# Where the first graph layer's accumulator clear, offset table, norm and state store run in a two-block graph kernel

## What is computed

```
x_in = layernorm(x)                               # the state, 3125 x 256
ew = edge_attr @ edge_w + edge_b                  # 100000 x 256
for l in range(3):
    residual = x_in
    msg = relu(x_in[src] * ew)
    out = 0
    for i in range(3):                            # edge types
        h = segment_sum(msg * (type == i), dst) / max(count_i, 1)
        out = out + h @ weights[l, i]
    out = out + x_in @ roots[l] + biases[l]
    x_in = residual + relu(out)
x = x + x_in
```

## Time and profile before

| | us |
|---|---|
| median of three runs | 7416.21 |
| the three runs | 7399.02, 7418.02, 7416.21 |
| profiled execution, device time | 7403.44 |
| its span in the trace | 7401.6 |

### The profile page before, as it was taken

The page is one execution under the profiler, slowest core; times in us unless marked ns, Lnnn a source line. Parts: engine busy times, 40 slices in busy tenths (PEclk is TensorE's granted clock), DMA queues, the critical chain, the costliest instruction groups (busy, mean ns, idle before and its releaser), DMA issues.

```text
span 7401.6 us, 95264 instructions
## 1 busy us (share of the span) xinstructions
PE 4706.3 (64%) x19009; PEld 2793.2 (38%) x19009; DVE 4623.4 (62%) x10963; ACT 2409.1 (33%) x5954; POOL 4497.2 (61%) x4196
## 2 busy tenths in 40 slices
PE   6599822223388887526676667666665766666588
PEld 2255411111244444314444436333333633333365
DVE  7877755555566667626666655666665566666553
ACT  0188700000166663014444442222221222222131
POOL 0000177777677778877777762777776277777600
PEclk9899955555599998758888878777776877777789
DMA  4000177777665553236666682666667376766700
GB/s 111 18 0 0 35 227 224 228 226 231 176 152 152 152 152 73 57 95 211 210 209 210 210 174 94 208 211 212 211 208 174 95 211 211 211 208 210 174 26 18
DMA packets 506841, 1150.06 MB, mean 155 GB/s; under 512 B 115695, under 2 KB 244306, under 8 KB 506497
## 3 DMA queue, kind: packets, MB, share of 16 engines
q0 software_dynamic: 187648, 458.07, 24.6%
q1 hardware_dynamic: 271844, 551.41, 22.5%
q10 hardware_dynamic: 47136, 138.12, 6.6%
HBM read 864.81 MB, written 281.13 MB: 155 GB/s over the span
## 4 chain that ended last, share of the span: by engine, by line
POOL 40%; issue 21%; PE 7%; DMA 4%; DVE 1%; POOLq 0%; ACT 0%; SPq 0%; DVEq 0%; ACTq 0%
POOL sort_mem L540 26%; POOL recB_d L513 14%; DMA sort_mem<-x_d,x_mem 4%; PE banks L1144 4%; PE banks L1039 1%; PE banks L1049 1%; PE banks L1134 1%; DVE xnt_mem L1345 0%; PE banks L1107 0%; POOLq L537 0%; POOL acc_mem L523 0%; DVE z_mem L1689 0%; POOL acc_mem L498 0%; DMA x_mem<-recB_d 0%; POOLq L119 0%
## 5 line engine op out<-in xcount | busy, mean ns | idle before, releaser
L540 POOL DMA_INDIRECT sort_mem<-x_d,x_mem x2568 | 2636.8, 1027 | 838.6 <-issue 796.9
L1107 PE MATMUL banks<-z_mem 128*128 128x257 f32 x5136 | 2065.4, 544 | 1192.6 <-DVE acc_mem L1507 1072.4
L1107 PEld LDWEIGHTS banks<-z_mem 128*128 128x128 f32 x5136 | 1168.8, 257 | 2075.8 <-DVE acc_mem L1507 1475.9
L1507 DVE TENSOR_TENSOR acc_mem<-acc_mem,banks 128x257 f32 x3376 | 1420.8, 421 | 528.5 <-PE banks L1107 162.5
L779 ACT ACTIVATE z_mem<-z_mem 128x512 f32<-128x512 f32 x1284 | 790.3, 631 | 2388.8 <-DVE z_mem L1689 2388.7
L498 POOL DMA_INDIRECT acc_mem<-h_d,z_mem x808 | 813.7, 1007 | 1135.5 <-ACTq L631 890.9
L1689 DVE TENSOR_TENSOR z_mem<-x_mem,sort_mem 128x512 f32<-128x512 f32 x1284 | 833.2, 691 | 961.3 <-DMA sort_mem<-x_d,x_mem 955.2
L513 POOL DMA_INDIRECT recB_d<-sort_mem x800 | 1010.5, 1263 | 270.5 <-issue 270.5
L954 PE MATMUL banks<-ident,z_mem 128*128 128x128 f32 x808 | 225.1, 434 | 728.0 <-DVE z_mem L1446 728.0
L1005 PE MATMUL banks<-acc_mem,z_mem 128*128 128x257 f32 x1616 | 545.5, 420 | 143.2 <-DVE acc_mem L1507 123.1
L937 PE MATMUL banks<-xnt_mem,acc_mem 125*128 125x512 f16 (+1 forms) x3200 | 549.2, 335 | 0.0
(11 more groups left out here) (274 smaller groups left out, 4786.6 us busy)
## 6 DMA issues: line engine op xcount, KB each, us to landing
x_mem<-ew_d SPq DMA_DIRECT2D x428, 512.0 KB, 4.2
ew_d<-x_mem SPq DMA_DIRECT2D x214, 512.0 KB, 3.0
pay_d<-acc_mem SPq DMA_DIRECT2D x202, 516.0 KB, 4.3
acc_mem<-pay_d ACTq DMA_DIRECT2D x202, 516.0 KB
x_mem<-recB_d SPq DMA_DIRECT2D x642, 68.0 KB
sort_mem<-x_d,x_mem POOLq DMA_INDIRECT x2568
edge_d<-xnt_mem ACTq DMA_DIRECT2D x40, 332.0 KB
sort_mem<-edge_d SPq DMA_DIRECT2D x40, 332.0 KB
```

Source lines behind the costliest of these rows:

```text
L540: pool.indirect_dma_start(out=xg[h % XG][:, k, :], out_offset=None, in_=x_d, in_offset=bass.IndirectOffsetOnAxis(ap=reci[h][:, k, W_SRC:W_ ...
L1107: m.matmul(bank[5 + tile % 3][:, :AC], oneh[:, Q % 2, k, :], msg[:, Q % 2, k, :], start=True, stop=True)\
L1507: v.tensor_tensor(a_, a_, bank_[:, :AC], ALU.add).then_inc(flushed, 1)
```

## The change

VectorE clears the whole of `acc_mem`, right after `layer_norm(3)`, in place of GpSimd. `layer_norm(3)` no longer stands behind the clear or behind the offsets. The offsets are unpacked after the clear, in a place of `x_mem` instead of `sort_mem`, behind `x2_moved`. SyncE waits for the four `edges_put` counts itself before it loads the first records. Its reload of x at the end of the layers waits also for the last flush, since `winB` now lies in the memory that this reload writes.

```diff
-        winB = sort_mem[0:1, 16 * D:16 * D + TB].bitcast(INT32)
+        winB = x_mem[0:1, 16 * D + TURN * 4 * RW:16 * D + TURN * 4 * RW + TB].bitcast(INT32)
...
                 if l == 0:
-                    sp.wait_ge(S("edge_w_ready"), 1)
+                    for u in range(4):
+                        sp.wait_ge(S(f"edges_put{u}"), BODIES // 4 * 320)
                     sp.wait_ge(S("x2_moved"), 16)
...
             sp.wait_ge(S("rec_turned"), QB)
+            sp.wait_ge(S("flushed_b"), LAYERS * TB)
             sp.dma_start(x_sb, x2_d.rearrange("(t p) d -> p t d", p=P)).then_inc(S("x2_moved"), 16)
...
                 if l == 0:
-                    pool.wait_ge(S("x2_ready"), 1)
                     for u in range(4):
                         pool.wait_ge(S(f"edges_put{u}"), BODIES // 4 * 320)
-                    g.memset(acc_mem, 0.0).then_inc(S("acc_zeroed"), 1)
...
             st.did(v.memset(msg[:, :, :, D:AC], 1.0))
-            dve.wait_ge(S("acc_zeroed"), 1)
-            for k in range(4):
-                st.run(v.tensor_scalar(winB4[:, :, k], winpB, 7 * k, 127, ALU.logical_shift_right, ALU.bitwise_and))
-            st.did(v.tensor_scalar(winB, winB, float(AC), None, ALU.mult))
             st.settle()
             dve.sem_inc(S("edge_w_ready"), 1)
             layer_norm(3, xn, "state_ready", stats_made=True, group=5)
+            st.did(v.memset(acc_mem, 0.0))
+            dve.wait_ge(S("x2_moved"), 16)
+            for k in range(4):
+                st.run(v.tensor_scalar(winB4[:, :, k], winpB, 7 * k, 127, ALU.logical_shift_right, ALU.bitwise_and))
+            st.run(v.tensor_scalar(winB, winB, float(AC), None, ALU.mult))
```

## The result

| | us |
|---|---|
| changed kernel, median of 10 runs | 7394.35 (7387.56 to 7413.34) |
| kernel before, median of 10 runs | 7414.97 (7399.02 to 7422.65) |
| ratio, 95% interval | 0.9977 (0.9967 to 0.9986) |
| profiled execution of the changed kernel, device time | 7413.34, span 7411.5 |

By the ratio the change made the kernel faster by 17 us (10 to 24); the medians lie 20.6 us apart. The forecast gain was 29.5 us. The profiled execution is the slowest of the ten, 19.0 us over their median, so its span is no measure of the gain; the stages in it are. Set beside the profile before, it takes some 8 us longer ahead of the seam and 11.1 us longer in the layers: 3743.4 us from the first gather's start to the last one's, against 3732.3.

A forecast was written before the change was run, and what follows sets the result against it. GpSimd's chain of waits was taken to bound the kernel, with a serial 33.7 us seam between scatters and gathers. The base of 7409.2 us less 29.5 gave 7379.7, predicted as 7380 us, range 7362 to 7400.

The forecast's parts named there:

- The seam is serial, and its inputs exist early: From last scatter to first gather: 33.7 us with one engine working at a time; VectorE's last small operand ready at 3128.7.
- The gain of 29.5 us: At the seam: the first record load goes out at 3236.1 instead of 3265.62 us, everything after it unchanged.
- Norm, stores, SyncE's queue, the wait at the end: Beside scatters, norm and stores cost nothing with 79 us slack; the final x reload costs 0 with 24.7 us slack.
- 0 to 1 us that I had allowed: At the first record load: possible further gain from an empty queue, taken as 0.
- The clear on VectorE, 16.4 us: Beside the scatters: twice the half clear's 8.20 us, running from 3140.4 to 3156.8, with 79 us slack.
- Do the moved VectorE operations hold up the scatters?: Norm, clear and offsets beside the scatters from 3128.7 us: claimed to cost GpSimd 0, called the one real unknown.
- The bound of 29.6 us: Most the moved work could cost the scatters: its full duration, 10.9 for norm, 16.4 for clear, 2.3 for offsets.
- The base: Whole kernel before the change: mean of four executions, 7409.2 us, expected between 7395 and 7418.
- Rival 1: At the scatters: moved VectorE work costs 17.9 us, leaving a gain of 11.6 and a time of 7397.6; chance 0.10.
- my range: For the whole kernel's time: 7362 to 7400 us, stretched from 7364.5 to 7390.8 to reach into rival 1.
- rival 3: In the layers: VectorE's 642 offset reads from x_mem are dearer; at 0.1 us each, 7443.9 us; chance 0.04.
- Rival 2: At the seam: no shortening, as moved work costs all 29.6 us or another input is late; 7409 us; chance 0.04.

The follow-up runs named there:

- g3: Changed kernel plus a wait between clear and first offset instruction, last 80 scatters held until x2_ready, against the kernel before: 7369.2 us, ratio 0.9961.
- h1: Changed kernel plus only a wait between VectorE's clear and the first offset instruction, no scatters held, against the kernel before: 7374.7 us, ratio 0.9955.
- h2: Changed kernel unaltered, timed again against the kernel before in the fourth group of runs: 7391.4 us, ratio 0.9983.
- g1: Kernel before with GpSimd's last 80 scatters held until x2_ready, against the kernel before without that hold: 7393.2 us, ratio 0.9997.
- g2: Changed kernel with GpSimd's last 80 scatters held until x2_ready, against the kernel before: 7382.9 us, ratio 0.9985.
- the first two groups: Follow-up runs of the changed kernel and variants in clear, wait or stores, against kernels before of 8273 and 8497.9 us; changed kernel ratios 1.0001 and 0.9994.
- held pair: g2 and g3: changed kernel without and with the wait behind the clear, last 80 scatters held until x2_ready: 7382.9 and 7369.2 us.
- e4: Changed kernel with VectorE clearing the accumulator twice in a row, the first clear awaited, against the kernel before: ratio 1.0009.
- i1: Changed kernel, last 80 scatters held until x2_ready, with a norm tensor_scalar issued behind the clear and offsets waiting for it: 8352.7 us, one run.
- i2: Changed kernel, last 80 scatters held until x2_ready, with a tensor_copy issued behind the clear and offsets waiting for it: 8338.6 us, one run.
- g4: Changed kernel, last 80 scatters held until x2_ready, with an 8-column reduce issued behind the clear and offsets waiting for it: 7359.8 us, one run.
- g5: Changed kernel, last 80 scatters held until x2_ready, with an 8-column two-input addition behind the clear and offsets waiting for it: 7370.2 us, one run.
- e7: Changed kernel plus a wait between the clear and the first offset instruction, against a kernel before of 8497.9 us: ratio 0.9999.
- e1: Changed kernel unaltered, run again in the first group against a kernel before of 8273 us: ratio 1.0001.
- e6: Changed kernel with SyncE issuing the five state stores only after all scatters have landed, kernel before 8497.9 us: 8509.0 us, one time.
- e8: Changed kernel unaltered, run again in the second group against a kernel before of 8497.9 us: ratio 0.9994.
- e2_clear_gpsimd: Changed kernel, but GpSimd clears the accumulator after the last scatter as before, against a kernel before of 8273 us: ratio 0.9997.
- the third group: Follow-up runs g1, g2, g3 and g4 with the last 80 scatters held until x2_ready, against a kernel before of 7393.7 us.

## Why the prediction was wrong

- **The seam is serial, and its inputs exist early:** right. All moved work was over by 3172 us in the profiled run, and from the last scatter's start to the first gather the seam shrank from 36.6 to 5.9 us.
- **The gain of 29.5 us:** right as the size of what the move removes. 30.8 us in the profile, and 29 and 33 us by the ratios (24.5 and 30.6 by the medians) where no scatter is stretched (g3, h1).
- **Norm, stores, SyncE's queue, the wait at the end:** right. The scatters beside the norm took 1.18 or 1.19 us, and beside the state stores none was stretched where no offset stood in line (g3, h1). The record load landed 1.3 us sooner, a little beyond the 0 to 1 us that I had allowed. At the end the reload of x was issued at 7040.90, landed 12.8 us later, and was first used at 7077.27.
- **The clear on VectorE, 16.4 us:** the row says 16.34, but the engine is taken for 4.25 + 16.34 = 20.6 us. I read the 2.10 us of "issue" before the half clear in the earlier trace rows as idle time. It belongs to the clear, for it grows with it: 1.34 us ahead of a memset of 6682 columns in the profile before, 2.10 at 9766, 4.25 at 19532.
- **"Do the moved VectorE operations hold up the scatters?" I take 0:** this is the step that failed. I priced each moved operation by a row of its own kind and did not ask what stands behind it. In the earlier trace rows a wait stands behind the clear. In the changed kernel `st.did` does not wait, the wait for `x2_moved` has been met (x landed 15.5 us after 3129.46), and the first offset operation is in line at once. The scatter that GpSimd begins 1.7 us later gets no further until the clear is over: 18.9 us, where I had put 0. With one wait in between the loss is gone (h1 against h2: 7374.7 against 7391.4 us). The bound of 29.6 us that I had written down covered it; the value that I took did not.
- **The base:** I took 7409.2 us from four executions. The ten of the result have a median of 7414.97, 5.8 us more, so even the full gain would have ended near 7385 and not at 7380.
- **Rival 1** had the right place, VectorE's moved work beside the scatters, and at the share of the earlier trace rows a loss of 17.9 us and a time of 7397.6 us, near the measured 18.9 and 7394.35, but by luck: it spread the loss over all 29.6 us of moved work, and its base was 5.8 us too low. The norm's operations held none while they ran (scatters of 1.18 or 1.19 us); an offset operation did so while it waited. That the measured time lies in my range is no support for the forecast either, since I had drawn the range out into this rival.
- **Rivals 2 and 3:** rival 3 did not happen. From its first gather to the second layer's first, the first layer takes 1294.4 us in g1, 1296.3 in g2 and 1295.1 in g3. Rival 2 is what the first two groups showed, ratios of 1.0001 and 0.9994 for the changed kernel, for a reason that I had not listed: there the second block, not the scatters, ends the seam. Their intervals are wide (the second reaches down to 0.9972), so a small gain is not excluded.

## What to carry to other kernels

When a long VectorE operation is put beside GpSimd's DMAs, look at the next VectorE instruction as well: here a copy or a `tensor_scalar` issued behind a memset without a wait kept GpSimd out until the memset's end (indirect DMAs of 20.04 to 20.69 us where they began early in it). The wait cost VectorE next to nothing (with it the first offset operation starts 0.04 us after the memset's end in h1, without it 0.08 us before it in h2) and gave 17 us (14 in the held pair, both by the medians). And find out which of two stages ends a seam before pricing it; in other executions of the same kernel it was the other one.

## What the runs showed of the hardware

- A `tensor_scalar` or copy in line behind a memset of 20.6 us stretched one indirect DMA of GpSimd from 1.18 (or 0.95) to 20.04 to 20.69 us, in six profiles (the changed kernel, e4, g2, h2, i1, i2); a reduce, an addition of 8 columns or a wait in its place, never (g4, g5, g3, h1, e7: at most 1.19 us for a scatter and 0.99 for a gather beside the memset). In the program no scatter waits for a semaphore of this memset, so the two engines do not meet only at semaphores, as the first section has it. Where the first gather started late in the memset (e1, e6, e8), it took 3.49 to 3.78 us and ended 1.0 us after it.
- The stretched DMA was the first that began 0.95 us or more after VectorE had taken the memset (its row's start less the gap ahead of it). A scatter that began 0.2 us after it (3149.37 in the changed kernel) ran whole.
- A VectorE memset occupied the engine for its row and the gap ahead of it: 16.34 + 4.25 us at 19532 columns, 8.20 + 2.10 at 9766, 5.63 + 1.34 at 6682.
- It goes the other way too. In `e2_clear_gpsimd` a cast of VectorE that takes 0.29 us in `e1_again` stood beside GpSimd's clear for its whole length (timelines of GpSimd and VectorE):

```profile
3508.54 16.38 POOL L525 MEMSET acc_mem<- 128x19532 f32 x1 [210.97 <-DVEq L1637]
3508.71 16.35 DVE L1641 CAST z_mem<-z_mem 128x256 bf16<-128x256 f32 x1
```

- The kernel before took 7415, 8273 and 8498 us (medians) in different groups of runs. In the profile of `e1_again` the DMA engines moved 158 to 197 GB/s in the page's slices that lie whole within a layer, where they moved 208 to 212 in the profile before, and the mean granted TensorE clock was 0.731 against 0.786. What sets the groups apart is not shown: the record gives the same chip number to the third group (7394 us) and to i1 and i2 (8276 us).
- What makes the two-input operations of the earlier trace rows stretch a scatter, when the small addition of g5 in line does not, was not tried.
